# The first gate folded into the value-output weights, and the second layernorm applied by ScalarE

## What is computed

```
x = x + tanh(g_xattn[0]) * xattn(layernorm(x), ctx, Wq, Wk, Wv, Wo, bo)
x = x + tanh(g_ffn[0])   * ffn(layernorm(x), w_gate, w_up, w_down)

xattn: softmax(qh kh^T / 8) vh over 16 heads, then @ Wo + bo
ffn:   h = silu(fp4(x) @ fp4(w_gate)^T) * (fp4(x) @ fp4(w_up)^T);  fp4(h) @ fp4(w_down)^T
layernorm: (x - mean) / sqrt(var + 1e-5), no weights
fp4: blocks of 16 along the last dim, scale = max|x| / 6, rounded to the E2M1 grid
```

## Time and profile before

| | us |
|---|---|
| median of three runs | 597.64 |
| lowest and highest | 597.33, 598.23 |
| the profiled execution, device time | 598.33 |
| its span, first to last instruction | 596.1 |

### The profile page before, as it was taken

One profiled execution on the slowest core, in us unless ns is written; L12 is line 12 of the kernel. 1 busy time (PEld: TensorE's weight loads), 2 busy tenths in 40 slices (PEclk: granted clock), 3 DMA queues, 4 the chain that ended last, 5 costly groups with the idle time before them and its releaser, 6 DMA issues.

```text
span 596.1 us, 9833 instructions
## 1 busy us (share of the span) xinstructions
PE 543.8 (91%) x2841; PEld 335.7 (56%) x2841; DVE 476.7 (80%) x793; ACT 312.3 (52%) x723; POOL 276.3 (46%) x234
## 2 busy tenths in 40 slices
PE   5889999999999998999999998999999999999642
PEld 4655565666566554666466554665566565656331
DVE  2769875889977996889977995789977997787655
ACT  3434756575456645575456644566456745546211
POOL 4007344553828173553828173363827264456400
PEclk9779999999999999999999999999999999999675
DMA  8500000200020000200020000200020000000000
GB/s 158 99 1 1 1 1 0 52 2 1 1 58 2 0 2 9 50 0 0 1 56 1 0 0 9 50 0 0 1 56 1 0 0 5 1 1 1 1 3 3
DMA packets 27892, 9.31 MB, mean 16 GB/s; under 512 B 24016, under 2 KB 27600, under 8 KB 27856
## 3 DMA queue, kind: packets, MB, share of 16 engines
q1 hardware_dynamic: 27856, 8.92, 7.5%
HBM read 8.50 MB, written 0.41 MB: 15 GB/s over the span
## 4 chain that ended last, share of the span: by engine, by line
PE 59%; DVE 27%; issue 10%; ACT 2%; DMA 1%; DVEq 0%; POOL 0%; SPq 0%; POOLq 0%; ACTq 0%
PE attn L789 16%; PE scores L775 11%; PE ring L728 10%; DVE max L897 8%; PE scores L776 7%; PE ring L735 4%; PE ring L742 4%; DVE f_abs L362 3%; DVE f_abs L364 2%; DVE e_gate L860 2%; DVE acc_v L919 2%; PE ring L707 2%; DVE h_fp L366 1%; DVE z L871 1%; DVE rsum L904 1%
## 5 line engine op out<-in xcount | busy, mean ns | idle before, releaser
L634 ACT ACTIVATE probs<-scores 120x400 f32<-120x400 f32 (+1 forms) x384 | 190.0, 504 | 211.7 <-PE scores L776 209.1
L897 DVE TENSOR_REDUCE max<-ring 116x1 f32<-116x482 f32 (+1 forms) x336 | 204.7, 649 | 28.4 <-PE ring L728 24.1
L505 POOL TENSOR_TENSOR acc_p<-acc_p,probs 120x800 f32<-120x800 f32 x79 | 156.3, 1978 | 61.7 <-ACT probs L634 58.1
L789 PE MATMUL attn<-probs,ctx_n 120*64 120x400 f32 (+1 forms) x768 | 173.9, 532 | 0.0
L775 PE MATMUL scores<-q_hh,k_hl 128*120 128x400 f32 (+1 forms) x384 | 155.0, 404 | 1.2 <-DVE q_ls L899 1.2
L775 PEld LDWEIGHTS scores<-q_hh,k_hl 128*120 128x120 f32 (+1 forms) x384 | 70.9, 185 | 128.2 <-ACT probs L634 70.2
L776 PE MATMUL scores<-q_ls,k_h 71*120 71x400 f32 (+1 forms) x384 | 134.8, 351 | 0.0
L728 PE MATMUL ring<-k_hl,q_hh 128*116 128x482 f32 (+1 forms) x336 | 119.6, 409 | 12.4 <-DVE max L897 4.7
L776 PEld LDWEIGHTS scores<-q_ls,k_h 71*120 71x120 f32 (+1 forms) x384 | 71.6, 186 | 4.2
L728 PEld LDWEIGHTS ring<-k_hl,q_hh 128*116 128x116 f32 (+1 forms) x336 | 59.1, 182 | 25.7 <-DVE max L897 9.9
L789 PEld LDWEIGHTS attn<-probs,ctx_n 120*64 120x64 f32 (+1 forms) x768 | 38.3, 136 | 46.4 <-issue 34.3
(11 more groups left out here) (127 smaller groups left out, 526.9 us busy)
## 6 DMA issues: line engine op xcount, KB each, us to landing
ctx_n<-in_ctx SPq DMA_DIRECT2D x16, 360.0 KB
wq<-in_L_xattn_Wq SPq DMA_DIRECT2D x1, 512.0 KB, 4.6
wo<-in_L_xattn_Wo SPq DMA_DIRECT2D x1, 512.0 KB, 6.8
x_in<-in_x SPq DMA_DIRECT2D x8, 50.0 KB
out<-y_out SPq DMA_DIRECT2D x8, 50.0 KB
wk<-in_L_xattn_Wk SPq DMA_DIRECT2D x1, 256.0 KB, 4.1
ctx_n<-in_ctx SPq DMA_DIRECT2D x16, 1.0 KB
wv<-in_L_xattn_Wv SPq DMA_DIRECT2D x1, 256.0 KB, 6.3
```

The costliest lines, as they stand in the source:

```text
L505: pool.tensor_tensor(acc_p[0:r, t.g % 2, :], left, probs[0:r, c % PROBS, :], ALU.add).then_inc(sum_p, 1)
L634: act.activation(probs[0:r, c % PROBS, k * HALF:(k + 1) * HALF], scores[0:r, slot % SCORE_BANKS, 0:HALF], ACT.Exp).then_inc(probs_full, 1)
L789: mm = pe.matmul(attn[64 * i:64 * i + C, k, 0:HALF], ctx_n[0:r, par, c, 0, :], probs[0:r, c % PROBS, k * HALF:(k + 1) * HALF], start=(j == ...
L897: dve.tensor_reduce(max3[0:rows, tile, part:part + 1], src[0:rows, 0:MAXC[part + 1] - MAXC[part]], AX.X, ALU.max).then_inc(free, 1)
```

## The change

tanh of the first gate is multiplied into `vo` when ScalarE copies it in the setup (the scale of the ACTIVATE), so DVE's multiplication of the inverse sums is left out. The bias `bo` is multiplied by the gate as before. DVE's step of the second layernorm in slot 17 is left out; instead GpSimd makes `offset` = -mean * rstd with two small multiplications right behind rstd, and ScalarE makes z = rstd * y + offset in one ACTIVATE, behind its ring reads of slot 17. In `finish` the same: GpSimd, then ScalarE ahead of its read of `zT`.

```diff
-LN2_SLOTS = [12, 13, 17]
+LN2_SLOTS = [12, 13]
+LN2_APPLY_SLOT = 17
...
+            pool.memset(minus_one[:, :], -1.0)
...
+            def ln2_rows(t):
+
+                rstd_of(stats[:, 1, :], 1, ln2_stats, 2 * t.batch(), ln2_eps, ln2_rstd, t.batch())
+                pool.wait_ge(ln2_rstd, t.batch())
+                pool.tensor_tensor(offset[0:N, :], stats[0:N, 1, 6:7], rstd[0:N, 1:2], ALU.mult).then_inc(ln2_mean, 1)
+                pool.wait_ge(ln2_mean, t.batch())
+                pool.tensor_tensor(offset[0:N, :], offset[0:N, :], minus_one[0:N, :], ALU.mult).then_inc(ln2_offset, 1)
...
                     if c == 7 and t.g % 2 == 0 and t.g >= 2:
-                        rstd_of(stats[:, 1, :], 1, ln2_stats, 2 * t.batch(), ln2_eps, ln2_rstd, t.batch())
+                        ln2_rows(t)
...
                 elif kind == "vo":
                     view = vo[:, :, :].rearrange("p (j r) n -> p r j n", r=2)
-                    act.activation(view[:, k % 2, 4 * (k // 2):4 * (k // 2) + 4], src.rearrange("p (j n) -> p j n", n=D), ACT.Copy).then_inc(free, 1)
+                    act.wait_ge(gates_set, 1)
+                    act.activation(view[:, k % 2, 4 * (k // 2):4 * (k // 2) + 4], src.rearrange("p (j n) -> p j n", n=D), ACT.Copy, scale=tanh_x[:, 0:1]).then_inc(free, 1)
...
+            def ln2_apply(t):
+
+                act.wait_ge(ln2_offset, t.batch())
+                act.activation(z[0:N, :], y[0:N, t.parity(-1), :], ACT.Identity, bias=offset[0:N, :], scale=rstd[0:N, 1:2]).then_inc(ln2_done, 1)
...
                     for key in ring_keys(t.g, slot):
                         ring_use(t, key)
+                    if t.g % 2 == 0 and t.g >= 2 and slot == LN2_APPLY_SLOT:
+                        ln2_apply(t)
...
                 for key in FINISH:
+                    if key[0] == "zT":
+                        ln2_apply(t)
                     ring_use(t, key)
...
                 elif kind == "sum":
-                    dve.reciprocal(rsum[0:N, :], src[0:N, 0:HG]).then_inc(norm_done, 1)
-                    dve.wait_ge(norm_done, t.count(1, 0))
-                    dve.tensor_scalar(rsum[0:N, :], rsum[0:N, :], tanh_x[0:N, :], None, ALU.mult).then_inc(free, 1)
+                    dve.reciprocal(rsum[0:N, :], src[0:N, 0:HG]).then_inc(free, 1)
...
-                else:
-                    dve.wait_ge(ln2_rstd, t.batch())
-                    ln_apply(y[0:N, par, :], z[0:N, :], stats[:, 1, :], 1, ln2_done)
```

More of the change, by code:

```diff
@@ L187, in xattn_ffn @@
         minus_half = sb("minus_half", [128, 1])
+        minus_one = sb("minus_one", [128, 1])
         eps = sb("eps", [128, 1])
@@ L235, in xattn_ffn @@
         rstd = sb("rstd", [128, 2])
+        offset = sb("offset", [128, 1])
         z = sb("z", [128, D])
@@ L275, in xattn_ffn @@
         sum_p = sem("sum_p")
-        norm_done = sem("norm_done")
         head_done = sem("head_done")
@@ L288, in xattn_ffn @@
         ln2_rstd = sem("ln2_rstd")
+        ln2_mean = sem("ln2_mean")
+        ln2_offset = sem("ln2_offset")
         ln2_done = sem("ln2_done")
@@ L946, in ln2 @@
                 par = t.parity(-1)
[L947 to L950, removed]
-                else:
-                    dve.wait_ge(ln2_rstd, t.batch())
-                    ln_apply(y[0:N, par, :], z[0:N, :], stats[:, 1, :], 1, ln2_done)
+                if step == 0:
+                    dve.wait_ge(head_done, t.count(4, 0))
+                ln_stats(step, y[0:N, par, :], stats[:, 1, :], ln2_stats, 2 * b)
             dve.wait_ge(x_loaded[0], 16)
@@ L1006, in finish @@
                         last_heads(t)
-                        for step in range(3):
+                        for step in range(2):
                             ln2(t, step)
```

## The result

The changed kernel takes 604.32 us (median of 18 runs, 598.97 to 608.88) against 597.91 for the kernel before (18 runs, 596.25 to 599.73) on the same chips: a ratio of 1.0093, with a 95% interval of 1.0065 to 1.0121. The ratio and its interval leave out the two longest of the 18 runs of the changed kernel (608.70 and 608.88), which lie over 1.5% above its fastest. The changed kernel is slower by about 1%; the forecast was 1.7% faster. The profiled execution took 607.48 us, its span is 605.6; it is one of the longer ones, 3.2 above the median, so of the 9.5 us that its span is above the one before (596.1) some 6 are there at the medians. Two things in these numbers ask for a reason: the sign, and the spread, which has grown from 3.5 to 9.9 us.

What follows compares the result with a forecast made beforehand. PE bounds even groups; in six odd groups PE loses time because DVE, held by a POOL add, frees banks late. -6.9 - 1.5 - 2.0 + 0.1 + 0.3 = -10.0 us, from 597.6 to 587.6; range 582.5 to 594.0.

Steps and rivals of the forecast that it cites:

- What bounds the kernel: Even groups are PE's; in six odd groups PE visibly loses 1.8 us, as DVE's L904 waits for POOL's add.
- about 1.1 and not 1.8: Sign of being right: in odd groups PE stands idle for about 1.1 us and not 1.8.
- Part 1, slot 8: Odd groups, slot 8: without L904 banks come free sooner, so it becomes as short as the even group's: 6 x 1.15 = 6.9 us.
- their start is paced by PE's maxima, so this wait moves with PE and stays: Odd groups, slot 19: the fp4 links ahead of the hidden rows' transpose (L752) move with PE, so its wait stays.
- the next ones are no victims: Odd groups: with L904 gone, L860 (one input) and L897 (reads PSUM) should not take over its 1.77 us stall.
- Rival (a): The wait only moves: group 15's chain keeps its length and slot 4's 0.25 us stays; 591.1 us, chance 22%.
- rival b: Group 15 gains more: PE standing for 1.2 us only could keep the clock, 3 to 5 us back; 582.3 us, chance 13%.
- Part 2: Layernorm step L871 leaves DVE: the hidden 0.25 us in the next odd group's slot 4, 6 x 0.25 = 1.5 us; 0 elsewhere in the loop.
- Group 15: The fp4 chain before L752, behind PE's 4.53 us wait, shortens by 0 to 3.3 us; 2.0 taken.
- `finish`: Everything serial: L904 goes, -0.27; two POOL steps add 0.5 to 0.6; ScalarE's 0.37 replaces DVE's 0.34; sum +0.3 us.
- Rival (d): Identity needs another table than Exp, so ScalarE reloads tables in even groups and at the end: +19.4 us, 607, chance 3%.
- The rule of the Trainium skill that was weighed against the change: A GpSimd instruction's lock blocks two-port or two-SBUF-input DVE instructions; a removed victim may hand on the wait, group 15 2.0 us higher.

Runs made afterwards that it cites:

- e2: Kernel before with only the layernorm step moved to GpSimd and ScalarE, the gate's multiplication left on DVE: 596.13 us, ratio 0.9971.
- e9: Changed kernel with fp4 links 0 to 5 in slot 7 and links 6, 7, 8 in slots 10, 12, 14: 581.96 us, ratio 0.9732.
- e11: Changed kernel with fp4 links 0 to 5 in slot 7 and links 6, 7, 8 in slots 9, 11, 13: 591.70 us, ratio 0.9890.
- e3: Changed kernel with four added matmuls of 482 columns, result overwritten, ahead of PE's slot 19 wait for the fp4 links: 592.67 us, ratio 0.9911.
- e12: Changed kernel with fp4 links 0-5 in slot 7, 6-8 in slots 10, 12, 14, and four added matmuls ahead of L752: 586.97 us, ratio 0.9809.

## Why the prediction was wrong

- **What bounds the kernel**: the reading held in the main. Even groups inside a pass of the loop stayed at PE's 31.3 us where the clock was up, the losses are in the odd groups, and L904's 1.77 us ended with GpSimd's add. But of the 1.8 us for which PE can be seen idle in group 7, 1.12 lay ahead of L752 and only 0.65 in slot 8; the sign "about 1.1 and not 1.8" fits slot 8's part going and the other staying. Group 3 of the changed kernel shows 2.3 (34.90 less 32.64).
- **Part 1, slot 8**: -6.9 us was right where it was read. The distance is 1.41, to the digit that of the even group. That the second reciprocal would not be held came true too, though no row of the prediction had shown it beside a chunk add: it takes 1.20 from 278.95, beside the add of 278.92 to 280.82.
- **The step that failed** is the one behind it: "their start is paced by PE's maxima, so this wait moves with PE and stays". The hidden rows didn't move with PE. They come through links held by GpSimd one after the other; DVE coming 1.4 to 1.7 us earlier changed which links are held, and lost 1.73 us to it (5.85 to 7.58). The transpose stayed 29.4 us behind the start of its group while PE came 1.0 us sooner. The prediction applied the lock to the instruction that was removed and to its nearest neighbours ("the next ones are no victims") but not to the nine links behind, though it names them as standing against later adds, and the trace of the kernel before has links 6 and 7 at 1.84 and 1.65. Rival (a), that the wait only moves, was the right mechanism; it had been granted for group 15 alone, where the trace shows less of it than feared.
- **The clock** was only named for a gain (rival b). The 1.12 us wait ahead of L752 grew to 2.11, and behind it the clock fell in five of six odd groups. "A PE that stands for 1.2 us only could keep the clock" agrees with the odd groups before, where no fall follows the waits of 1.06 to 1.12; it was not asked the other way round for the six groups where the wait would double, and the sum has no term for it. The term is +12.2 us (two of its seven falls lie at the loop's border, one more than before), and turns what would have been a small gain into a loss.
- **Part 2**: 0.25 us per odd group was right (e2 has 0.3; in slot 4 of the changed kernel `gate` to the next start is 0.55, 273.64 to 274.19). ScalarE's ACTIVATE takes 486 ns (x8), not the 0.37 taken from L593. It has two operands from tiles and reads SBUF, L593 has one and reads PSUM; no run tells which of these makes the difference. In the loop this was covered, as forecast; GpSimd's two multiplications took 190 ns each. ScalarE waited for `offset` once in the loop, 0.34 us in group 14.

```profile
L640 ACT ACTIVATE z<-y,offset,rstd 100x128 f32<-100x128 f32 x8 | 3.9, 486 | 8.0 <-POOL offset L469 8.0
L467 POOL TENSOR_TENSOR offset<-stats,rstd 100x1 f32<-100x1 f32 x8 | 1.5, 190 | 0.6
```

- **Group 15** was forecast at -2.0 and `finish` at +0.3. PE's wait there fell from 4.53 to 1.81, and the transpose starts 23.25 us into the group (568.45 from 545.20) instead of 26.51 (559.21 from 532.70): 3.3 sooner. The fp4 chain begins 1.95 earlier, and the scaling of a few columns passes ahead of the add and takes 0.18 instead of 1.68, both as forecast. The clock still fell right behind the 1.81 us (scores at 0.54 from 570.60), for 6.8 us instead of 10.2; so rival (b)'s condition, a wait of 1.2, was not reached. From the start of group 15 to the end the span shrank by 3.0. In `finish`, the last statistics to the first fp4 link take 2.17 us (584.21 to 586.38) where they took 1.49 (575.43 to 576.92), with 0.27 won on the gate: +0.4 for a forecast +0.3. So group 15 gained 3.4, just beyond its 0 to 3.3, some of it the clock's.

```profile
556.50 0.18 DVE L356 TENSOR_SCALAR f_small<-f_small 100x22 f32<-100x22 f32 x1
...
568.45 0.36 PE L775 MATMUL ring<-ident,h_fp 100*128 100x100 f32 x2 [1.81 <-DVE h_fp L370]
```

- **Rival (d)**, the slower side, was of the wrong kind: the profile after has one ACT_TABLE_LOAD, in the setup (L621, x1). As the Trainium skill has it (ScalarE: Activation LUTs, Table sets: the hidden batching unit), Identity needs no other table; here the trace agrees.
- The rule of the Trainium skill that was weighed against the change (SBUF — State Buffer, Who interferes with whom) is the one that decided. The trace agrees with it for the links too: 1.58 and 1.88 us where 0.52 and 0.34 are plain. It should have been followed down DVE's whole queue to the next thing that PE waits for.

This is what became of the expected 1.4 us per odd group: it was won in slots 4 and 8, given back ahead of the transpose of slot 19 (an odd group at full clock has 34.9 us before and after), and paid for a second time by the clock.

## What to carry to other kernels

Freeing time on an engine whose instructions are held by another engine's moves everything behind it. Before the gain is counted, list the next instructions of that queue that can be held, up to the one which the bounding engine waits for, and see which of the other engine's instructions they will meet at their new times. A wait that grows, even where the sum of waits stays the same, has to be priced with TensorE's clock: one wait of 2.1 us cost more here than waits of 0.25, 1.15 and 1.1. When a freed engine gives nothing, the schedule around it may have been tuned to its old lateness, as here: the change and a new order together (e9: 0.9732) were worth what neither was alone (1.0093 and 1.0024).

## What the runs showed of the hardware

- The clock can fall behind a wait of 2.1 us on PE, and doesn't always: in the trace of the changed kernel it stayed at full speed behind the wait of group 3, and fell behind the same wait in groups 5, 7, 9, 11 and 13. It also fell behind waits of 1.81 (group 15) and 1.71 (e11, group 7), and behind none of the six of 1.06 to 1.12 in the kernel before. The changed kernel's spread goes along with it in the main: executions with a mean clock of 0.959 have spans of 597.2 and 597.5 us, those with 0.938 have 605.1 and 605.2.
- Added work that is thrown away made the kernel 11 us faster (e3), and 5 us slower where there was no wait to fill (e12).
- DVE instructions of several kinds are held beside a GpSimd add: a scaling of 8 columns (1.77 us for 0.23), a scalar_tensor_tensor (1.84 for 0.52), a tensor_tensor (2.26 for 0.52). The maxima read from PSUM (0.65) and the reciprocals (1.20) kept their usual time beside the adds.
